# Cross-attention with a gated FP4 feed-forward: the loop over groups written out, the rounding chain for h moved behind the maxima, its transposes and the down product moved into the next group

## What is computed

```python
def xattn(q, kv):                      # 16 heads of 64
    qh, kh, vh = q @ Wq, kv @ Wk, kv @ Wv          # split into heads
    attn = softmax(qh @ kh.T / 8)                  # 100 x 1444 for each head and batch
    return (attn @ vh) @ Wo + bo

def fp4(a):                            # blocks of 16 along the last axis
    scale = max(abs(a)) / 6            # of each block, at least 1e-12
    return nearest of (0, .5, 1, 1.5, 2, 3, 4, 6) to abs(a) / scale, * sign(a) * scale

def ffn(x):                            # w_gate, w_up: 352 x 128, w_down: 128 x 352
    h = silu(fp4(x) @ fp4(w_gate).T) * (fp4(x) @ fp4(w_up).T)
    return fp4(h) @ fp4(w_down).T

x = x + tanh(g_xattn) * xattn(layernorm(x), ctx)
x = x + tanh(g_ffn) * ffn(layernorm(x))
```

## Time and profile before

| | us |
|---|---|
| median of the 3 runs | 604.34 (601.37 to 604.54) |
| the profiled execution's own time | 607.48 |
| its span, first to last instruction | 605.6 |
| PE busy | 553.8 |
| DVE busy | 456.6 |
| ACT busy | 315.3 |
| POOL busy | 275.1 |
| mean granted TensorE clock | 0.945 |

### The profile page before, as it was taken

The page is one execution under the profiler, slowest core; times in us unless marked ns, Lnnn a source line. Parts: engine busy times, 40 slices in busy tenths (PEclk is TensorE's granted clock), DMA queues, the critical chain, the costliest instruction groups (busy, mean ns, idle before and its releaser), DMA issues.

```text
span 605.6 us, 9832 instructions
## 1 busy us (share of the span) xinstructions
PE 553.8 (91%) x2841; PEld 343.7 (57%) x2841; DVE 456.6 (75%) x769; ACT 315.3 (52%) x731; POOL 275.1 (45%) x251
## 2 busy tenths in 40 slices
PE   5889999999899988999899997999899998999842
PEld 4655565756465645656466654656466565656421
DVE  2769865789877994689857895779966897677645
ACT  3444646575366644575346743566455753556311
POOL 4008353645528280554617272282806364184600
PEclk9979999999999997999989998899989997999875
DMA  9500000200020000200020000200010000000000
GB/s 157 96 1 1 1 1 1 50 2 2 3 54 2 1 1 8 49 0 1 0 56 1 0 1 8 49 0 1 0 41 16 0 0 4 2 1 1 4 0 3
DMA packets 27892, 9.31 MB, mean 15 GB/s; under 512 B 24016, under 2 KB 27600, under 8 KB 27856
## 3 DMA queue, kind: packets, MB, share of 16 engines
q1 hardware_dynamic: 27856, 8.92, 7.6%
HBM read 8.50 MB, written 0.41 MB: 15 GB/s over the span
## 4 chain that ended last, share of the span: by engine, by line
PE 72%; DVE 19%; issue 4%; ACT 2%; DMA 1%; POOL 1%; SPq 1%; ACTq 0%; POOLq 0%; DVEq 0%
PE attn L812 21%; PE scores L798 15%; PE ring L751 10%; PE scores L799 10%; DVE max L920 7%; PE ring L765 4%; PE ring L758 3%; PE ring L730 2%; DVE f_t L364 2%; DVE f_abs L368 2%; DVE f_abs L360 2%; PE ring L737 2%; PE ring L779 1%; PE ring L771 1%; DVE h_fp L370 1%
## 5 line engine op out<-in xcount | busy, mean ns | idle before, releaser
L653 ACT ACTIVATE probs<-scores 120x400 f32<-120x400 f32 (+1 forms) x384 | 190.3, 504 | 212.4 <-PE scores L799 209.5
L920 DVE TENSOR_REDUCE max<-ring 116x1 f32<-116x482 f32 (+1 forms) x336 | 205.3, 651 | 38.1 <-PE ring L751 35.3
L518 POOL TENSOR_TENSOR acc_p<-acc_p,probs 120x800 f32<-120x800 f32 x79 | 154.5, 1955 | 65.2 <-ACT probs L653 61.6
L812 PE MATMUL attn<-probs,ctx_n 120*64 120x400 f32 (+1 forms) x768 | 177.7, 543 | 0.0
L798 PE MATMUL scores<-q_hh,k_hl 128*120 128x400 f32 (+1 forms) x384 | 158.4, 412 | 1.2 <-DVE q_ls L922 1.2
L798 PEld LDWEIGHTS scores<-q_hh,k_hl 128*120 128x120 f32 (+1 forms) x384 | 72.5, 189 | 131.0 <-ACT probs L653 67.6
L799 PE MATMUL scores<-q_ls,k_h 71*120 71x400 f32 (+1 forms) x384 | 137.6, 358 | 0.0
L751 PE MATMUL ring<-k_hl,q_hh 128*116 128x482 f32 (+1 forms) x336 | 119.1, 410 | 8.0 <-ACT q_hh L588 4.1
L799 PEld LDWEIGHTS scores<-q_ls,k_h 71*120 71x120 f32 (+1 forms) x384 | 73.7, 192 | 4.2
L751 PEld LDWEIGHTS ring<-k_hl,q_hh 128*116 128x116 f32 (+1 forms) x336 | 58.8, 183 | 19.4 <-DVE max L920 6.9
L812 PEld LDWEIGHTS attn<-probs,ctx_n 120*64 120x64 f32 (+1 forms) x768 | 38.9, 138 | 47.7 <-issue 36.6
(11 more groups left out here) (129 smaller groups left out, 521.7 us busy)
## 6 DMA issues: line engine op xcount, KB each, us to landing
ctx_n<-in_ctx SPq DMA_DIRECT2D x16, 360.0 KB
wq<-in_L_xattn_Wq SPq DMA_DIRECT2D x1, 512.0 KB, 4.2
wo<-in_L_xattn_Wo SPq DMA_DIRECT2D x1, 512.0 KB, 7.3
x_in<-in_x SPq DMA_DIRECT2D x8, 50.0 KB
out<-y_out SPq DMA_DIRECT2D x8, 50.0 KB
wk<-in_L_xattn_Wk SPq DMA_DIRECT2D x1, 256.0 KB, 3.6
ctx_n<-in_ctx SPq DMA_DIRECT2D x16, 1.0 KB
wv<-in_L_xattn_Wv SPq DMA_DIRECT2D x1, 256.0 KB, 6.2
```

The lines of the kernel that those rows point to most:

```text
L518: pool.tensor_tensor(acc_p[0:r, t.g % 2, :], left, probs[0:r, c % PROBS, :], ALU.add).then_inc(sum_p, 1)
L653: act.activation(probs[0:r, c % PROBS, k * HALF:(k + 1) * HALF], scores[0:r, slot % SCORE_BANKS, 0:HALF], ACT.Exp).then_inc(probs_full, 1)
L812: mm = pe.matmul(attn[64 * i:64 * i + C, k, 0:HALF], ctx_n[0:r, par, c, 0, :], probs[0:r, c % PROBS, k * HALF:(k + 1) * HALF], start=(j == ...
L920: dve.tensor_reduce(max3[0:rows, tile, part:part + 1], src[0:rows, 0:MAXC[part + 1] - MAXC[part]], AX.X, ALU.max).then_inc(free, 1)
```

## The change

The loop is gone: all 16 groups are written out on every engine, and `Turn` loses its register. The nine links of the rounding chain for h move from slots 7 to 16 of the odd group to slots 18 to 23. The transposes of h and the down product, with ACT's copies, DVE's y_out operation and SP's store, move into the next, even group: slots 2, 3 and 5 (`DOWN_SLOTS`). The order in which the ring's banks are used follows. Only group 15 keeps the old slots for all of it (`LAST_FFN_SLOTS`, `LAST_H_SLOTS`), since no group comes after it; the transposes of the weights in group 1 keep their slots too. Nothing in what is computed changes.

```diff
--- before.py
+++ after.py
@@ -64,8 +64,10 @@
 
 
 MAX_SLOTS = {1: 1, 2: 1, 4: 1, 5: 2, 7: 3, 8: 2, 10: 2, 11: 2, 12: 1, 13: 2, 14: 1, 15: 1, 16: 1, 17: 1}
-FFN_SLOTS = {2: ('zT', 0), 4: ('gate', 0), 6: ('up', 0), 19: ('hT', 0), 20: ('hT', 1), 22: ('down', 0)}
-W_SLOTS = {slot: ("wT", i) for i, slot in enumerate(FFN_SLOTS)}
+FFN_SLOTS = {2: ('zT', 0), 4: ('gate', 0), 6: ('up', 0)}
+DOWN_SLOTS = {2: ('hT', 0), 3: ('hT', 1), 5: ('down', 0)}
+LAST_FFN_SLOTS = {**FFN_SLOTS, 19: ('hT', 0), 20: ('hT', 1), 22: ('down', 0)}
+W_SLOTS = {slot: ("wT", i) for i, slot in enumerate(LAST_FFN_SLOTS)}
 POST_SLOTS = {6: ('sum', 0), 8: ('proj', 0), 10: ('proj', 1)}
 CTX_SLOTS = {14: ('ctx', 0), 15: ('ctx', 1), 18: ('ctx', 2)}
 XT_SLOT = 20
@@ -77,7 +79,8 @@
 LN2_APPLY_SLOT = 17
 Z_SLOTS = [19, 19, 20, 21, 21, 21, 22, 22, 22]
 SIGMOID_SLOTS = [5, 6]
-H_SLOTS = [7, 8, 9, 10, 11, 12, 13, 14, 16]
+H_SLOTS = [18, 19, 19, 20, 21, 21, 22, 22, 23]
+LAST_H_SLOTS = [7, 8, 9, 10, 11, 12, 13, 14, 16]
 ADD_LAG, LAST_ADD_SLOT = 3, 0
 
 
@@ -86,8 +89,9 @@
     pre = g + 1 < GROUPS
     if pre and slot == 0:
         keys += [("q", 0)]
-    if g % 2 and slot in FFN_SLOTS:
-        keys += [(FFN_SLOTS if g >= 3 else W_SLOTS)[slot]]
+    ffn = W_SLOTS if g == 1 else LAST_FFN_SLOTS if g == GROUPS - 1 else FFN_SLOTS if g % 2 else DOWN_SLOTS if g >= 4 else {}
+    if slot in ffn:
+        keys += [ffn[slot]]
     if g % 2 == 0 and g + 2 < GROUPS and slot in CTX_SLOTS:
         keys += [CTX_SLOTS[slot]]
     if g >= 1 and slot in POST_SLOTS:
@@ -128,45 +132,40 @@
 
 
 RING = number_ring()
-RING_PER_LOOP = RING[(6, ("q", 0))] - RING[(2, ("q", 0))]
-assert RING_PER_LOOP % RING_BANKS == 0
-for _g in range(1, 10):
-    for _s in range(SLOTS):
-        for _k in ring_keys(_g, _s):
-            if _k[0] != "wT":
-                assert RING[(_g + 4, _k)] - RING[(_g, _k)] == RING_PER_LOOP
-
 
 class Turn:
 
 
-    def __init__(self, g, p=0):
-        self.g, self.p = g, p
+    def __init__(self, g):
+        self.g = g
 
     def count(self, per_group, plus):
 
-        return per_group * self.g + plus + (4 * per_group) * self.p
+        return per_group * self.g + plus
 
     def batch(self, ahead=0):
 
-        return self.g // 2 + ahead + 2 * self.p
+        return self.g // 2 + ahead
 
     def parity(self, ahead=0):
         return (self.g // 2 + ahead) % 2
 
     def fills(self, ahead=0):
 
-        return (self.g // 2 + ahead) // 2 + 1 + self.p
+        return (self.g // 2 + ahead) // 2 + 1
 
     def ring(self, key):
 
         i = RING[(self.g, key)]
-        assert self.g >= 1 or isinstance(self.p, int)
-        return i % RING_BANKS, i // RING_BANKS + 1 + (RING_PER_LOOP // RING_BANKS) * self.p
+        return i % RING_BANKS, i // RING_BANKS + 1
+
+    def down_batch(self):
+
+        return self.batch(-1 if self.g % 2 or self.g == GROUPS else -2)
 
     def before(self):
 
-        return Turn(self.g - 1, self.p)
+        return Turn(self.g - 1)
 
 
 def xattn_ffn(nc, x, ctx_in, g_xattn, g_ffn, Wq, Wk, Wv, Wo, bo, w_gate, w_up, w_down, out):
@@ -330,12 +329,7 @@
 
         def all_groups(engine, group, finish):
 
-            for g in (0, 1):
-                group(Turn(g))
-            with engine.Fori(0, (GROUPS - 4) // 4) as p:
-                for g in (2, 3, 4, 5):
-                    group(Turn(g, p))
-            for g in (GROUPS - 2, GROUPS - 1):
+            for g in range(GROUPS):
                 group(Turn(g))
             finish(Turn(GROUPS))
 
@@ -417,7 +411,8 @@
             sp.dma_start(w_raw[:, 6 * D:], w_down).then_inc(ffn_in, 16)
 
             def store(t):
-                b, par = t.batch(-1), t.parity(-1)
+                b = t.down_batch()
+                par = b % 2
                 wait_reads(sp, (t, ("down", 0)))
                 sp.dma_start(out[b, :, :], y_out[0:N, par, :]).then_inc(stored[par], 16)
 
@@ -431,7 +426,7 @@
                     if t.g >= 2:
                         sp.wait_ge(pv_done, t.count(12, 0))
                     load_ctx(t.batch(1), t.parity(1))
-                if t.g % 2 and t.g >= 3:
+                if t.g % 2 == 0 and t.g >= 4 or t.g == GROUPS - 1:
                     store(t)
 
             def finish(t):
@@ -770,7 +765,7 @@
                     wait_reads(pe, (t, ("zT", 0)), own=bank)
                     mm = pe.matmul(dst[0:N, 0:F], zT[:, :], (gateT if kind == "gate" else upT)[:, :], start=True, stop=True)
                 elif kind == "hT":
-                    pe.wait_ge(hq4, LINKS * t.batch())
+                    pe.wait_ge(hq4, LINKS * (t.down_batch() + 1))
                     for i in (0, 1) if k == 0 else (2,):
                         mm = pe.transpose(dst[0:FT[i], (i % 2) * N:(i % 2 + 1) * N], h_fp4[0:N, 128 * i:128 * i + FT[i]], ident[0:N, 0:N])
                 elif kind == "down":
@@ -924,8 +919,8 @@
                 elif kind == "sum":
                     dve.reciprocal(rsum[0:N, :], src[0:N, 0:HG]).then_inc(free, 1)
                 elif kind == "down":
-                    par = t.parity(-1)
-                    dve.wait_ge(stored[par], 16 * t.fills(-1))
+                    par = t.down_batch() % 2
+                    dve.wait_ge(stored[par], 16 * (t.down_batch() // 2 + 1))
                     dve.scalar_tensor_tensor(out=y_out[0:N, par, :], in0=src[0:N, 0:D], scalar=tanh_f[0:N, :], in1=y[0:N, par, :],
                                              op0=ALU.mult, op1=ALU.add).then_inc(free, 1)
 
@@ -1008,13 +1003,14 @@
                     if not even and t.g >= 3:
                         if slot in SIGMOID_SLOTS:
                             sigmoid(t, SIGMOID_SLOTS.index(slot))
-                        if slot in H_SLOTS:
-                            h_fp4_link(t, H_SLOTS.index(slot))
+                        slots = LAST_H_SLOTS if t.g == GROUPS - 1 else H_SLOTS
+                        for link in [i for i in range(LINKS) if slots[i] == slot]:
+                            h_fp4_link(t, link)
                     if t.g == 0 and slot in (3, 4, 5, 11, 12, 14, 22):
                         weights_fp4(dve, {3: 0, 4: 1, 5: 2, 11: 4, 12: 5, 14: 6, 22: 8}[slot])
 
             def finish(t):
-                add(Turn(t.g - 1, t.p), CHUNKS - 1)
+                add(t.before(), CHUNKS - 1)
                 add_last(t)
                 for key in FINISH:
                     if key[0] == "proj":
```

## The result

The changed kernel takes **573.24 us** (median of 4 runs, 571.3 to 575.98) against 604.12 for the kernel before in the runs beside it: a ratio of 0.950, 95% interval 0.945 to 0.955. The profiled execution took 572.5 with a span of 570.7, against 607.48 and 605.6.

What follows compares the result with a forecast made beforehand. PE was taken to set the pace. Removing 29.9 us (waits for h 12.6, jumps 6.9, lowered clock 10.4) and adding 6.6 of new wait gave -23.3, 584.2 from 607.48; the forecast was 583, range 577 to 597.

Steps and rivals of the forecast that it cites:

- The bound: PE, busy 553.8 of 605.6 us with 72% of the chain, sets the pace; DVE matters only where PE waits.
- the waits for h: PE's waits before the transposes of h at slot 19: 2.10 us in six odd groups, 12.6 to be removed.
- the jumps: The loop's jumps back, before groups 6 and 10: two at 3.43 us, 6.9 removed by writing the loop out.
- up for removal: Groups 3 to 13: 29.9 us, made of 12.6 waits for h, 6.9 jumps and 10.4 lowered clock.
- What stretches the links: POOL's adds stretch DVE's links of h's chain; in slots 18 to 23 links 3 to 8 take 0.35 to 0.55.
- Link 1 held to S + 1.1: DVE's link 1 held until POOL's adds end, 1.1 us after shift matmul start S; PE then waits 1.05.
- The template: Even group 4 of the earlier kernel: POOL's adds end at S + 1.1, PE's slot 2 ring use at S + 6.55.
- the walk: DVE's steps timed from link 1 to link 8 at S + 7.45; with 0.05 for DVE's lag, 1.1 a pair, 6.6 in all.
- no wait: Rival: link 1 gets in before POOL's last add, so the 6.6 us go too: 577 us, chance 0.10.
- Group 15 at nothing: Group 15 keeps its chain in place and the end after it is untouched: 0 us.
- The sum: -29.9 + 6.6 = -23.3 us, clock staying up: 584.2 from the profiled execution's 607.48.
- The price of a jump: Group 6, beginning with a jump back, against group 4: 34.76 - 31.33 = 3.43 us.

Runs made afterwards that it cites:

- the POOL experiments: Changed kernel with three more POOL adds in groups 3 to 13: 617.74 us; earlier kernel, loop written out, POOL adding 8 of 800 columns of chunks 5 to 8: 571.22.
- eight columns: Earlier kernel with its loop written out, POOL adding only 8 of 800 columns of chunks 5 to 8 in groups 3 to 13: 571.22 us, ratio 0.950.
- the kernel with one jump: Changed kernel with groups 4 to 11 in a loop of two turns, one jump back left between groups 7 and 8: 576.89 us, ratio 0.960.
- the chain back: Changed kernel with the nine links back in slots 7 to 16, transposes and down product still in the next group: 611.68 us, ratio 1.014.

## Why the prediction was right and wrong

**The bound, the waits for h, the jumps: right.** The 2.1 us waits are gone in six groups, and with them the slow clock; the groups of one kind are all alike. The windows of groups 3 to 13 give up 32.7, where 29.9 were up for removal and another 1.3 left the stretch with group 13's transposes and down product (an even group that has them takes 32.61 instead of 31.33).

**What stretches the links: right.** That POOL's adds do it, and that they would not in slots 18 to 23, was read off the rows; the POOL experiments confirm it from both sides, with adds added (+44 us) and taken away (the old order as fast as the new). One reading was off: link 3, at 149.12, does not lie inside the four adds from 152.37 on but beside POOL's products of `head_out` (149.04 to 151.83). These stay with eight columns, and so does its length (1.62).

**Link 1 held to S + 1.1: wrong, and this is the step that failed.** The prediction had POOL done at S + 1.1, as in group 4, and link 1 0.35 behind the boundary between POOL's last two adds. In the changed kernel POOL was done at S + 1.37 (160.14 against the shift at 158.77), its fourth add started at S - 0.52, and link 1 at S - 0.60. The template was 0.3 off and the walk about 0.1, and these decided between 0 and 1.1 us a pair, 6.6 us in all. Most of the template's error has a cause that the prediction put at nothing: group 4 of the kernel before lies inside the loop, where POOL's adds follow each other at 0.08 us, and written out they follow at 0.14, 0.2 more over the three gaps up to the fourth add. In the kernel with one jump POOL is done at S + 1.12 to S + 1.17 in the loop's odd groups and at S + 1.34 and S + 1.40 in groups 13 and 3 outside it. The walk itself was sound: with link 0 done twice PE waits 0.73 plus 0.16 more for a bank, and the kernel takes 580.3. The rival "no wait" had this mechanism with a chance of 0.10, for two points as close as that against template and rounding it deserved a third or more.

**Group 15 at nothing: wrong by about 3.** In the earlier trace rows its wait was counted among the seven, but I summed the lowered clock for groups 3 to 13 alone. In the kernel before, group 15's down product ran at the low level; in the changed one the wait is the same and the clock stays (the first line is from before, the others from after):

```profile
571.60 1.48 PE L779 MATMUL ring<-downT,hT 128*100 128x128 f32 x6
...
536.61 0.36 PE L770 MATMUL ring<-ident,h_fp 100*128 100x100 f32 x2 [1.82 <-DVE h_fp L364]
...
539.02 0.82 PE L774 MATMUL ring<-downT,hT 128*100 128x128 f32 x6
```

From the first transposes of group 15 to the end of the span it takes 34.1 instead of 37.2 (536.61 to 570.7, 568.45 to 605.6), and PE is busy for 14.7 instead of 17.8 with the same 79 matmuls: the 3.1 are clock alone. Why it stays here and fell there is open. The down product of group 15 takes 1.48 or 1.49 behind the same wait in the kernels with only the loop written out, with the chain back, with link 0 twice and with one jump, 1.23 with three more POOL adds, and 0.82 with eight columns and in the second trace of the changed kernel.

**What a wait costs beyond its length: 1.6 more than forecast.** A pair takes 63.83 instead of the 64.10 of the undisturbed groups 3 and 4 of before; six pairs are 1.6. Short waits for a maximum's bank are not the reason: they were 0.14 to 0.20 in each odd group and are 0.20 to 0.21 in each even group now. But the 2.10 that I took out is only the time in which no matmul ran. The scores ahead of the transposes and the transposes themselves, in group 3, before (the transposes at 161.00) and with eight columns for POOL:

```profile
158.55 0.35 PE L799 MATMUL scores<-q_ls,k_h 71*120 71x400 f32 x1
...
157.98 0.35 PE L795 MATMUL scores<-q_ls,k_h 71*120 71x400 f32 x1
158.16 0.34 PE L771 MATMUL ring<-ident,h_fp 100*128 100x100 f32 x2
```

Without a wait the second starts 0.18 after the first, while that one still runs; with the wait it is 2.45. So the wait costs 2.27, which is 0.17 of the 0.27 a pair. The rest of it is open.

**The sum** by these corrections: 584.2 - 6.6 - 3.1 - 1.6 = 572.9 against 572.5 in the profiled execution.

**The price of a jump: the whole right, the parts wrong.** It is 1.9 by itself and took 1.5 more in lowered clock where the clock fell. And the loop is worth little alone (5.4 us): as long as the waits of 2.1 stay, the lowered clock costs 10.4 in groups 3 to 13 of the trace of before and about 15 in that with the loop written out, which is of a longer run. Once the waits are gone it is worth more than its jump: 0.83 in each even group behind a held link 1. Of the 35.0 us between the profiled executions, 12.7 are waits for h, 3.8 are the two jumps, 1.6 are what waits cost beyond their length and the open rest of it, and 16.5 are lowered clock (10.4 in groups 3 to 13, 3.0 behind the jumps, 3.1 in group 15); 0.4 is not assigned. The 10.4 and the 3.0 went together with the waits and jumps ahead of them; the 3.1 went although its wait stayed.

The Trainium skill says that GpSimd shares its SBUF interfaces with VectorE, in contention with VectorE instructions in a 2-port mode or with two SBUF inputs (GPSIMD Engine Reference, key points). The POOL experiments agree: links with two inputs take up to 2.17 instead of 0.53 beside POOL's adds. Links 1, 4 and 5, with one input, are held as well (1.6 to 2.0); whether they run in a 2-port mode no run shows. The Trainium skill also says that going from one block of straight code to the next is mostly hidden (Runtime: NRT & Kernel Launch, instruction fetch mechanics), and the traces agree: the written-out groups from 3 to 13 of one kind are alike to 0.05 us.

## What to carry to other kernels

Before moving a chain of small vector operations, look at what POOL does beside it: the same nine operations took 4.05 us after the last group, and six of them alone 7.6 in group 3 of before. Then ask which step of the chain falls on a boundary between two of POOL's instructions; a step that gets by with 0.05 us should be moved to where being held costs nothing. Take such a template from code of the same form: POOL's adds lay 0.06 us further apart in straight code than in the loop. And count PE's short waits with the clock that falls behind them: here the second part was about as large as the first.

## What was not expected of the hardware

DVE's one-number-per-block operation (22 values a row, 0.18 us) is held for up to 1.9 us by a POOL add that has started, in one case only 0.02 us earlier (group 7 with link 0 done twice), but not by one that starts 0.05 us later: it gets in between two adds that follow each other directly. It ends 0.03 to 0.04 after the add that held it.

POOL takes 0.14 us from one add to the next in straight code and 0.08 in the loop.

Waits of PE of 0.7 to 1.0 us had no fall of the clock behind them in six of six cases; those of 1.8 in group 15 had in six kernels and not in the two traces of the changed one and with eight columns; those of 2.1 to 2.4 had in five of six, both before and with the loop written out; those of 2.7 and 4.2 in six of six. What decides it in between stays open.
